# The second layer's sorted feed-forward with its first product turned round, a third turn of store slack, and the loops written out

## The chip, the cores and the metric

The kernel runs on one core of one Trainium2 chip. The metric is the device time of one launch in microseconds (us). The kernel before takes 1609.66 us in the median of three runs (1603.33, 1609.66 and 1609.8).

## The reference

Four layers on 4096 tokens of width 128, each an attention against a context followed by a feed-forward. The change concerns the feed-forward of the second layer (`_L1_ffn_ref`), applied to the normalized x and added to it:

```python
router_probs = softmax(x_flat @ gate_w)                  # 8 experts
expert_idx = argmax(router_probs); expert_w = its probability
for e in range(8):
    h = gelu(x_flat @ w1[e] + b1[e], approximate=False)  # 128 -> 512
    y = h @ w2[e] + b2[e]                                # 512 -> 128
    out = out + where(expert_idx == e, expert_w, 0)[:, None] * y
```

All is float32. Each token needs one expert alone.

## The kernel before, in words

Every engine works through its own list of instructions in order; a `wait_ge` on a semaphore holds back all that stands behind it on that engine. The layer's feed-forward is built by `ffn1` (L1377) in three steps.

`route` computes the gates; its SyncE list loads w1, w2, b1 and b2 (b1 and b2 broadcast to all partitions, L747). `places` (L1087) sorts the tokens by expert on VectorE: each half of the tokens (16 tiles of 128) gets 24 blocks of 128 rows, and every block holds tokens of one expert only, so there are 48 blocks. `c.block_expert` has the expert of each block. `c.expert_pair` (L1184 to L1186) holds two experts in one number, that of a block and that of the block three earlier, for TensorE, which wants both in one turn.

`routed_gelu` (L1189) then runs:

- GpSimd scatters the token rows by indirect DMAs into `slots_x` (L1223, 32 of them). Once a half's results have all been stored it gathers them back from `slots_y` into `c.v` (L1231, 16 a half).
- SyncE loads one block a turn into one of four `xb` buffers (L1245) and stores the result of six blocks earlier (L1248).
- TensorE, in turn i: reads the expert pair from memory into a register (L1272), transposes block i (L1278), multiplies block i-1 with its expert's w1 (L1282: the block is the stationary operand, 512 columns of w1 move, the tokens come out on the partitions), turns the four 128-column parts of the Gelu's result of block i-3 (L1289), and multiplies block i-4 with w2 in four accumulating parts (L1295). Float32 products show as two matmul records each; transposes as one.
- ScalarE copies the transposed block (L1312), copies the turned hidden block (L1316), and takes the Gelu of 128x512 (L1321).
- VectorE adds the broadcast b1 to the 128x512 product (L1337), and b2 to the 128x128 result (L1345). Before each it reads the block's expert into a register (L1334, L1341).
- After its last block VectorE adds the gathered rows to x, times the gate (L1354), takes their statistics (L1358), and aggregates them with one instruction a tile (L1363, 32 of them).

`step` is written out by `run_steps` for the first and last turns and is otherwise a hardware loop of four turns. The lags are in one line:

```python
LAG = dict(X=0, UP=1, HT=3, Y=1 + PAIR_LAG, STORE=6)
```

`moments` (L96) makes mean and variance of all 32 tiles from the statistics with six instructions on all tiles at once (L101 to L109); the other layers use it.

Of the kernel before, what the change touches and what calls it, by code (L numbers as in the profile page):

```python
# [21 lines left out]
P = 128  # L22
# [12 lines left out]
PAIR_LAG = 3  # L35
# [1051 lines left out]
def places(nc, c, d):  # L1087
# [7 lines left out]
    with ExitStack() as own, nc.Block() as block:  # L1095
        numbers, ones, sel, ping, pong, share, over, blocks, ends, ends_b, start, slot, late, ids, pair = scratch(
# [5 lines left out]
                late=([1, HALVES, BLOCKS, EX], F32), ids=([1, HALVES, BLOCKS], F32),  # L1102
                pair=([1, HALVES * BLOCKS + PAIR_LAG], F32)))
# [17 lines left out]
        def _(dve):  # L1121
# [19 lines left out]
            nc.vector.memset(pair[:], 0.0)  # L1141
# [41 lines left out]
            NB = HALVES * BLOCKS  # L1183
            link(nc.vector.tensor_scalar(pair[:, PAIR_LAG:PAIR_LAG + NB], flat_ids, 8.0, None, ALU.mult))  # L1184
            link(nc.vector.tensor_tensor(pair[:, 0:NB], pair[:, 0:NB], flat_ids, ALU.add))
            nc.vector.tensor_copy(c.expert_pair[:], pair[:])  # L1186


def routed_gelu(nc, c, w):  # L1189
# [3 lines left out]
    CH, XB = 4, 4  # L1193
    HT, NB, FF = NT // HALVES, HALVES * BLOCKS, 512
    (xt_psum, xt_ready, h_psum, hb_ready, gelu_ready, ht_psum, ht_ready, y_psum, y_ready, added, stats_ready) = semaphores(
        nc, c, "e1", "xtp xt h hb gelu htp ht yp y add bn")
# [3 lines left out]
    y_out = semaphores(nc, c, "e1", "out0 out1")  # L1200
    xt_bank, h_bank, ht_bank, y_bank = ([c.bank[n], c.bank[n + 1]] for n in (0, 2, 4, 6))
    FIRST, U, LOOPS, LAST = 4, 4, NB // 4 - 1, NB + 6
    LAG = dict(X=0, UP=1, HT=3, Y=1 + PAIR_LAG, STORE=6)
    TB = HT // 4

    def Block(i, r, lag=0):
        return Item(i - lag, r, U, NB)

    with ExitStack() as own, nc.Block() as block:
        xb, xT, hb, h, hT, y, stats = scratch(nc, own, "e1", dict(  # L1210
            xb=([P, XB, P], F32), xT=([P, 2, P], F32), hb=([P, 2, FF], F32), h=([P, 2, FF], F32),
            hT=([P, 2, CH, P], F32), y=([P, 2, P], F32), stats=([P, NT, 6], F32)))

        def rows(halves, a):

            half = a.n // BLOCKS
            return halves[half][bass.ds(a.items(P, -half * BLOCKS * P), P), :]

        @block.gpsimd
        def _(pool):  # L1220
# [4 lines left out]
            for half in range(HALVES):  # L1225
                pool.wait_ge(placed[half], 16 * HT)
                for k in range(2):

                    pool.wait_ge(y_out[k], 16 * (half + 1) * BLOCKS // 2 + 16)
                for j in range(half * HT, (half + 1) * HT):  # L1230
                    nc.gpsimd.indirect_dma_start(c.v[:, j, :], None, c.slots_y[half][:, :],  # L1231
                                                 bass.IndirectOffsetOnAxis(ap=c.slot[:, j:j + 1], axis=0)
                                                 ).then_inc(back[j // TB], 16)

        @block.sync
        def _(sp):
            for s in y_out:
                sp.sem_inc(s, 16)

            def step(i, r):  # L1240
                x, yy = Block(i, r), Block(i, r, LAG["STORE"])
                if x.live:
                    if x.n >= XB:
                        sp.wait_ge(xt_psum, x.items(1, -1))
                    sp.dma_start(xb[:, x.n % XB, :], rows(c.slots_x, x)).then_inc(block_in[x.n % XB], 16)  # L1245
                if yy.live:
                    sp.wait_ge(y_ready, done(yy.t))
                    sp.dma_start(rows(c.slots_y, yy), y[:, yy.b, :]).then_inc(y_out[yy.b], 16)  # L1248

            sp.wait_ge(placed[0], 16 * HT)  # L1250
            run_steps(sp, step, 2 * U, U, BLOCKS // U - 2, BLOCKS)
            sp.wait_ge(placed[1], 16 * HT)
            for i in range(BLOCKS, BLOCKS + 2 * U):
                step(i, 0)
            with sp.Fori(0, BLOCKS // U - 2) as r:
                for n in range(U):
                    step(BLOCKS + 2 * U + n, r)
            for i in range(NB, LAST):
                step(i, 0)
            for s in y_out:  # L1260
                sp.wait_ge(s, 16 * NB // 2 + 16)

        @block.tensor
        def _(pe):
            for s in (xt_psum, h_psum, ht_psum, y_psum):
                pe.sem_inc(s, 2)

            def step(i, r):
                x, up, ht, yy = (Block(i, r, LAG[k]) for k in ("X", "UP", "HT", "Y"))

                if up.live or yy.live:
                    both = pe.value_load(c.expert_pair[0:1, bass.ds(up.t, 1)], min_val=0, max_val=63)  # L1272
                    y_expert = (both >> 3) & 7
                    up_expert = both & 7
                if x.live:
                    pe.wait_ge(block_in[x.n % XB], r * 16 + (16 * (x.n // XB) + 16))
                    pe.wait_ge(xt_ready, free(x.t))
                    nc.tensor.transpose(xt_bank[x.b][:, 0:P], xb[:, x.n % XB, :], c.ident[:]).then_inc(xt_psum, 1)  # L1278
                if up.live:
                    pe.wait_ge(xt_ready, done(up.t))  # L1280
                    pe.wait_ge(hb_ready, free(up.t))
                    nc.tensor.matmul(h_bank[up.b], xT[:, up.b, :],  # L1282
                                     w["w1"][:, bass.ds(up_expert, 1), :].rearrange("d a f -> d (a f)"),
                                     start=True, stop=True).then_inc(h_psum, 1)
                if ht.live:
                    pe.wait_ge(gelu_ready, done(ht.t))
                    pe.wait_ge(ht_ready, free(ht.t))
                    for k in range(CH):
                        last = nc.tensor.transpose(ht_bank[ht.b][:, k * P:(k + 1) * P], h[:, ht.b, k * P:(k + 1) * P], c.ident[:])  # L1289
                    last.then_inc(ht_psum, 1)  # L1290
                if yy.live:
                    pe.wait_ge(ht_ready, done(yy.t))
                    pe.wait_ge(y_ready, free(yy.t))
                    for k in range(CH):
                        last = nc.tensor.matmul(y_bank[yy.b][:, 0:P], hT[:, yy.b, k, :],  # L1295
                                                w["w2"][:, bass.ds(y_expert, 1), k * P:(k + 1) * P].rearrange("d a f -> d (a f)"),
                                                start=k == 0, stop=k == CH - 1)
                    last.then_inc(y_psum, 1)

            run_steps(pe, step, FIRST, U, LOOPS, LAST)  # L1300

        @block.scalar
        def _(act):
            for s in (xt_ready, gelu_ready, ht_ready):
                act.sem_inc(s, 2)

            def step(i, r):
                x, up, ht = (Block(i, r, LAG[k]) for k in ("X", "UP", "HT"))
                if x.live:
                    act.wait_ge(xt_psum, done(x.t))  # L1310
                    act.wait_ge(h_psum, free(x.t))
                    nc.scalar.activation(xT[:, x.b, :], xt_bank[x.b][:, 0:P], ACT.Identity).then_inc(xt_ready, 1)  # L1312
                if ht.live:
                    act.wait_ge(ht_psum, done(ht.t))
                    act.wait_ge(y_psum, free(ht.t))
                    nc.scalar.activation(hT[:, ht.b].rearrange("p k t -> p (k t)"), ht_bank[ht.b],  # L1316
                                         ACT.Identity).then_inc(ht_ready, 1)
                if up.live:
                    act.wait_ge(hb_ready, done(up.t))
                    act.wait_ge(ht_psum, free(up.t))  # L1320
                    nc.scalar.activation(h[:, up.b, :], hb[:, up.b, :], ACT.Gelu).then_inc(gelu_ready, 1)  # L1321

            run_steps(act, step, FIRST, U, LOOPS, LAST)
# [3 lines left out]
        def _(dve):  # L1327
            for s in (hb_ready, y_ready):
                dve.sem_inc(s, 2)

            def step(i, r):
                up, yy = (Block(i, r, LAG[k]) for k in ("UP", "Y"))
                if up.live:
                    e = dve.value_load(c.block_expert[0:1, bass.ds(up.t, 1)], min_val=0, max_val=7)  # L1334
                    dve.wait_ge(h_psum, done(up.t))
                    dve.wait_ge(gelu_ready, free(up.t))
                    nc.vector.tensor_tensor(hb[:, up.b, :], h_bank[up.b],  # L1337
                                            w["b1"][:, bass.ds(e, 1), :].rearrange("p a f -> p (a f)"),
                                            ALU.add).then_inc(hb_ready, 1)
# [678 lines left out]
```

## Time and profile before

| | before |
|---|---|
| median of three runs | 1609.66 us |
| the profiled execution itself | 1602.56 us |
| its span (first to last instruction) | 1600.6 us |
| TensorE matmul busy in the span | 1272.1 us (79%) |
| VectorE busy | 924.9 us (58%) |
| ScalarE busy | 639.6 us (40%) |
| mean granted TensorE clock | 0.86 of 2.4 GHz |
| first block load to last result of the changed loop | 652.4 to 773.8 us of the span |

The profile is of one execution. Busy times of engines overlap, so they don't add up to the span. The chain of waits that ended last covers only the last 40 us of the program (the final sums), so the changed stage must be read from its own stretch of the trace: by the busy time of each engine there, and by what each instruction waited for. DVE is VectorE, ACT is ScalarE, PE is TensorE's matmul and PEld its weight load, POOL is GpSimd, SP is SyncE.

### The profile page before, as it was taken

How to read it: one execution, taken by the hardware profiler on the slowest of the kernel's cores; microseconds unless marked ns; L12 is line 12 of the kernel's file. 1: busy time of each engine (PE TensorE's matmuls, PEld its weight loads, DVE VectorE, ACT ScalarE, POOL GpSimd, SP SyncE). 2: the span in 40 equal slices, each digit the busy share in tenths (PEclk: the TensorE clock that was granted, in tenths of full speed). 3: DMA queues.
4: the chain of work that ended last, by engine and by line, in shares of the span. 5: the costliest groups of instructions: out<-in, count | busy, mean ns of one | idle time of the engine just before them, and what ended most of it. 6: DMA issues, size and time to landing. Idle time of an engine off the chain costs nothing. (4 is left out here: it accounts for less than half of the span.)

```text
span 1600.6 us, 38656 instructions
## 1 busy us (share of the span) xinstructions
PE 1272.1 (79%) x13623; PEld 793.1 (50%) x13624; DVE 924.9 (58%) x2265; ACT 639.6 (40%) x1604; POOL 552.9 (35%) x1109
## 2 busy tenths in 40 slices
PE   3999986998999972699379999966699996864640
PEld 2566655665555552477245555534355555433420
DVE  6566655556677754244564555548657766494324
ACT  1266652222366641355123444431046664442210
POOL 2144412001255412503322334201635422646860
PEclk9799995999899985799688999988879996985555
DMA  5000002800000030212100000010000002142329
GB/s 182 1 3 3 3 2 73 250 1 1 1 2 3 2 157 26 76 54 82 41 1 2 2 2 2 3 54 1 0 2 2 2 2 64 40 171 43 53 36 262
DMA packets 84301, 68.46 MB, mean 43 GB/s; under 512 B 10608, under 2 KB 80048, under 8 KB 82992
## 3 DMA queue, kind: packets, MB, share of 16 engines
q1 hardware_dynamic: 75952, 56.88, 11.5%
q0 software_dynamic: 8192, 9.45, 3.1%
q8 instruction: 103, 1.69, 0.4%
q14 instruction: 54, 0.44, 0.1%
HBM read 42.00 MB, written 24.30 MB: 41 GB/s over the span
## 5 line engine op out<-in xcount | busy, mean ns | idle before, releaser
L481 DVE TENSOR_REDUCE a_m<-psum 128x4 f32<-128x512 f32 x512 | 329.7, 686 | 252.4 <-PE psum L386 99.0
L523 ACT ACTIVATE a_pt<-psum 128x512 f32<-128x512 f32 x512 | 307.2, 601 | 243.0 <-PE psum L414 243.0
L370 PE MATMUL psum<-h_kbd,h_qT 32*128 32x512 f32 x1024 | 323.5, 682 | 23.7 <-PEq L184 21.6
L379 PE MATMUL psum<-h_qbd,h_kT 32*128 32x512 f32 x1024 | 309.8, 659 | 0.0
L423 PE MATMUL psum<-a_pt,v_x 128*32 128x128 f32 x4096 | 165.6, 280 | 2.5 <-ACT a_pvs L531 2.1
L571 POOL CAST max_parts<-a_m 128x16 bf16<-128x16 f32 x128 | 25.1, 196 | 397.5 <-DVE a_m L481 397.5
L414 PEld LDWEIGHTS psum<-a_mt,minus_sb 32*128 32x128 bf16 x2048 | 85.4, 94 | 86.9 <-issue 72.1
L370 PEld LDWEIGHTS psum<-h_kbd,h_qT 32*128 32x128 f32 x1024 | 90.4, 194 | 71.1 <-issue 43.8
L423 PEld LDWEIGHTS psum<-a_pt,v_x 128*32 128x32 f32 x4096 | 96.9, 109 | 30.0 <-issue 4.4
L414 PE MATMUL psum<-a_mt,minus_sb 32*128 32x128 bf16 x2048 | 109.5, 217 | 0.0
L379 PEld LDWEIGHTS psum<-h_qbd,h_kT 32*128 32x128 f32 x1024 | 86.6, 188 | 3.9 <-issue 2.4
L386 PE MATMUL psum<-mask_sb,ident_rows 32*128 32x512 bf16 x1024 | 81.6, 384 | 0.0
L312 PE MATMUL psum<-ident_sb,p_xn 128*128 128x128 f32 x128 | 21.6, 295 | 72.6 <-DVE p_xn L201 72.5
L1337 DVE TENSOR_TENSOR e_hb<-psum,w_b 128x512 f32<-128x512 f32 x48 | 33.2, 692 | 66.8 <-PE psum L1282 66.1
L531 ACT ACTIVATE a_pvs<-psum 128x128 f32<-128x128 f32 x256 | 69.7, 272 | 2.2 <-PE psum L423 2.1
L595 POOL TENSOR_SCALAR h_kbd<-h_kT,head_of 128x512 f32<-128x512 f32 x96 | 65.2, 692 | 0.0
L595 POOL TENSOR_SCALAR h_qbd<-h_qT,head_of 128x512 f32<-128x512 f32 x96 | 65.2, 692 | 0.0
L1231 POOL DMA_INDIRECT v_sb<-slots_y,w_slot x32 | 30.5, 953 | 94.1 <-DMA slots_y<-e_y 84.9
L541 ACT ACTIVATE a_mt<-psum 128x128 bf16<-128x128 bf16 x128 | 35.4, 277 | 68.1 <-PE psum L444 67.0
L312 PEld LDWEIGHTS psum<-ident_sb,p_xn 128*128 128x128 f32 x128 | 16.4, 150 | 89.5 <-DVE p_xn L201 52.9
L386 PEld LDWEIGHTS psum<-mask_sb,ident_rows 32*128 32x128 bf16 x1024 | 34.2, 94 | 52.0 <-issue 38.0
L584 POOL COPY v_x<-v_sb 128x64 f32<-128x64 f32 x256 | 52.0, 236 | 15.2 <-PE psum L423 15.2
(262 smaller groups left out, 2597.2 us busy)
## 6 DMA issues: line engine op xcount, KB each, us to landing
sum_rows<-zero_row SPq DMA_DIRECT2D x1, 8320.0 KB, 37.1
end_sums<-sum_rows SPq DMA_DIRECT2D x16, 512.0 KB, 7.3
w_w<-in_f_w SPq DMA_DIRECT2D x2, 2048.0 KB, 9.9
w_up<-in_f_up SPq DMA_DIRECT2D x1, 4096.0 KB
slots_x<-zero_row SPq DMA_DIRECT2D x2, 1536.0 KB, 9.9
e_xb<-slots_x SPq DMA_DIRECT2D x48, 64.0 KB, 1.8
slots_y<-e_y SPq DMA_DIRECT2D x48, 64.0 KB
x_sb<-in_x SPq DMA_DIRECT2D x4, 512.0 KB, 6.0
```

What stands on the lines that cost most here:

```text
L312: last = nc.tensor.transpose(xt_bank[g % 2][:, j * P:(j + 1) * P], xn[:, g % 2, j, :], c.ident[:])
L370: return nc.tensor.matmul(score_bank[job % 3], c.qT[r, tokens(t)], c.kbd[r, t // GT % 2, :, within(t)], start=True, stop=not masked)
L379: nc.tensor.matmul(turned_bank[job % 3], c.kT[r, tokens(t)], c.qbd[r, t // GT % 2, :, within(t)], start=True, stop=False)
L386: return nc.tensor.matmul(bank, c.ident_rows[r, s, :], c.mask[r, side, s].rearrange("p h k -> p (h k)"), start=False, stop=stop)
L414: last = nc.tensor.matmul(turned_bank[(4 * st + n) % 3][:, j * P:(j + 1) * P], c.minus[r, j, :], mt[r, st % 2, :], start=False, stop=j == 3)
L423: last = nc.tensor.matmul(pv[32 * g:32 * g + 32, f, :], c.vx[:, t % 2, h, :], pt[:, t % 2, h, :], start=odd == 0, stop=odd == 1)
L481: nc.vector.reduce_max(m[:, t % 2, 4 * r:4 * r + 4], score_bank[job % 3].rearrange("p (h k) -> p h k", h=4), AX).then_inc(maxed, 1)
L523: nc.scalar.activation(pt[:, t % 2, 4 * r:4 * r + 4, :].rearrange("p h q -> p (h q)"), turned_bank[job % 3], ACT.Exp, scale=scale).then_in ...
L531: nc.scalar.activation(pvs[:, t % 2, f, :], pv[:, f, :], ACT.Identity).then_inc(pv_ready, 1)
L541: nc.scalar.activation(mt[:, t % 2, :], mt_turned, ACT.Identity).then_inc(mt_ready, 1)
L584: last = nc.gpsimd.tensor_copy(dst[:, :, odd, 16 * odd:16 * odd + HD], src[:, :, odd, :])
L595: last = nc.gpsimd.tensor_scalar(wide[:, g % 2, j, :], of[:, g * GN:(g + 1) * GN], c.head_of[:, j:j + 1], 1.0, ALU.mult, ALU.mult)
```

## The change

The first product is turned round: w1's four 128x128 parts are the stationary operands and the transposed block moves, so the hidden block comes out with its 512 features on the partitions, as the second product needs it. The four transposes of the hidden block and their ScalarE copy go. b1 then lies along the partitions and goes into the Gelu as its bias, four columns behind each expert's w1; the Gelu is four 128x128 instructions that read PSUM. Since the parts of w1 are now stationary operands with fixed addresses, VectorE copies the block's expert (128x516) into one of three `w1` buffers first. The result has three buffers (before two), the hidden block three. TensorE reads one expert a turn (the one for w2); the pairs go. All engines' turns are written out, without a hardware loop. At the end `moments` takes the place of the 32 aggregations.

```diff
 def places(nc, c, d):
...
-            nc.vector.memset(pair[:], 0.0)
...
             nc.vector.tensor_copy(c.block_expert[:], flat_ids)
-            link(nc.vector.tensor_scalar(pair[:, PAIR_LAG:PAIR_LAG + NB], flat_ids, 8.0, None, ALU.mult))
-            link(nc.vector.tensor_tensor(pair[:, 0:NB], pair[:, 0:NB], flat_ids, ALU.add))
-            nc.vector.tensor_copy(c.expert_pair[:], pair[:])
 def routed_gelu(nc, c, w):
-    CH, XB = 4, 4
+    CH, XB, YB, WB, HB = 4, 4, 3, 3, 3
...
+    UP_LAG, Y_LAG = 1, 3
...
+        def stored(b):
+            return 16 * ((b - b % YB) // YB + 1)
...
         def _(sp):
...
+            for b in range(NB + Y_LAG + 2):
+                if b < NB:
+                    if b % BLOCKS == 0:
+                        sp.wait_ge(placed[b // BLOCKS], 16 * HT)
+                    if b >= XB:
+                        sp.wait_ge(xt_psum, b - XB + 1)
+                    sp.dma_start(xb[:, b % XB, :], rows(c.slots_x, b)).then_inc(block_in[b % XB], 16)
+                k = b - Y_LAG - 2
+                if k >= 0:
+                    sp.wait_ge(y_ready, k + 1)
+                    sp.dma_start(rows(c.slots_y, k), y[:, k % YB, :]).then_inc(y_out[k % YB], 16)
...
         def _(pe):
...
+            for i in range(NB + Y_LAG):
+                if i < NB:
+                    pe.wait_ge(block_in[i % XB], 16 * (i // XB + 1))
+                    if i >= 2:
+                        pe.wait_ge(xt_ready, i - 1)
+                    nc.tensor.transpose(xt_bank[i % 2][:, 0:P], xb[:, i % XB, :], c.ident[:]).then_inc(xt_psum, 1)
+                b = i - UP_LAG
+                if 0 <= b < NB:
+                    pe.wait_ge(xt_ready, b + 1)
+                    pe.wait_ge(wide_ready, b + 1)
+                    if b >= 2:
+                        pe.wait_ge(gelu_ready, b - 1)
                     for k in range(CH):
+                        last = nc.tensor.matmul(h_bank[b % 2][:, k * P:(k + 1) * P], w1[:, b % WB, k * P:(k + 1) * P],
+                                                xT[:, b % 2, :], start=True, stop=True)
+                    last.then_inc(h_psum, 1)
+                b = i - Y_LAG
+                if b >= 0:
+                    e = pe.value_load(c.block_expert[0:1, b:b + 1], min_val=0, max_val=7)
+                    pe.wait_ge(gelu_ready, b + 1)
+                    if b >= 2:
+                        pe.wait_ge(y_ready, b - 1)
                     for k in range(CH):
+                        last = nc.tensor.matmul(y_bank[b % 2][:, 0:P], h[:, b % HB, k * P:(k + 1) * P],
+                                                w["w2"][:, bass.ds(e, 1), k * P:(k + 1) * P].rearrange("d a f -> d (a f)"),
                                                 start=k == 0, stop=k == CH - 1)
                     last.then_inc(y_psum, 1)
...
         def _(act):
...
+            for i in range(NB + UP_LAG):
+                if i < NB:
+                    act.wait_ge(xt_psum, i + 1)
+                    if i >= 2:
+                        act.wait_ge(h_psum, i - 1)
+                    nc.scalar.activation(xT[:, i % 2, :], xt_bank[i % 2][:, 0:P], ACT.Identity).then_inc(xt_ready, 1)
+                b = i - UP_LAG
+                if b >= 0:
+                    act.wait_ge(h_psum, b + 1)
+                    if b >= HB:
+                        act.wait_ge(y_psum, b - HB + 1)
+                    for k in range(CH):
+                        last = nc.scalar.activation(h[:, b % HB, k * P:(k + 1) * P], h_bank[b % 2][:, k * P:(k + 1) * P],
+                                                    ACT.Gelu, bias=w1[:, b % WB, FF + k:FF + k + 1])
+                    last.then_inc(gelu_ready, 1)
...
         def _(dve):
...
+            AHEAD = 2
+
+            def take_weights(b):
+                if b >= NB:
+                    return
+                if b >= WB:
+                    dve.wait_ge(gelu_ready, b - WB + 1)
+                e = dve.value_load(c.block_expert[0:1, b:b + 1], min_val=0, max_val=7)
+                nc.vector.tensor_copy(w1[:, b % WB, :], w["w1"][:, bass.ds(e, 1), :].rearrange("p a f -> p (a f)")
+                                      ).then_inc(wide_ready, 1)
+
+            for b in range(AHEAD):
+                take_weights(b)
+            for b in range(NB):
+                take_weights(b + AHEAD)
+                e = dve.value_load(c.block_expert[0:1, b:b + 1], min_val=0, max_val=7)
+                dve.wait_ge(y_psum, b + 1)
+                if b >= YB:
+                    dve.wait_ge(y_out[b % YB], stored(b - YB))
+                nc.vector.tensor_tensor(y[:, b % YB, :], y_bank[b % 2][:, 0:P],
+                                        w["b2"][:, bass.ds(e, 1), :].rearrange("p a f -> p (a f)"),
+                                        ALU.add).then_inc(y_ready, 1)
...
-            for j in range(NT):
-                nc.vector.bn_aggr(c.mv[:, j, :], stats[:, j, :])
+            moments(nc, c, dve, half_mean, links)
 def ffn1(nc, c, d):
...
-                               (b1[:], d["f1_b1"].partition_broadcast(P)), (b2[:], d["f1_b2"].partition_broadcast(P))])
+                               (b2[:], d["f1_b2"].partition_broadcast(P))])
```

The removed engine bodies are those of L1240 to L1349. GpSimd's gathers wait for the last three stores of a half (before: for both result buffers' counts). On the host `f1_w1` gets the four columns of b1 behind each expert's 512.

## Rows read from the trace of the kernel before

**Rows 1.** Two windows of the loop: us, each engine busy (x count), PEclk, DMA

```profile
667.00:720.00 53.00, 52.60 (x331) 39.35 (x330) 21.63 (x44) 28.72 (x66) 3.59 (x4) 1.00 0.21 61
720.00:772.00 52.00, 51.63 (x336) 39.58 (x334) 20.95 (x43) 28.66 (x64) 15.15 (x16) 1.00 0.26 72
```

**Rows 2.** Groups by line in the stretch 655 to 775 us, shapes apart

```profile
L1282 PE MATMUL psum<-w_w,e_xT 128*128 x96 | 52.6, 631 | 1.1 <-DVE e_hb L1337 0.4
L1295 PE MATMUL psum<-w_w,e_hT 128*128 x384 | 50.9, 276 | 0.3 <-issue 0.3
...
L1337 DVE TENSOR_TENSOR e_hb<-psum,w_b 128x512 f32<-128x512 f32 x48 | 33.2, 692 | 66.8 <-PE psum L1282 66.1 <-issue 0.7
...
L1289 PE MATMUL psum<-ident_sb,e_h 128*128 128x128 f32 x192 | 28.8, 273 | 0.0
...
L1312 ACT ACTIVATE e_xT<-psum 128x128 f32<-128x128 f32 x48 | 12.9, 270 | 43.8 <-PE psum L1278 43.8
```

**Rows 3.** Timeline of one turn: start us, us, engine, line, operation

```profile
703.28 0.60 PE L1289 MATMUL psum<-ident_sb,e_h 128*128 128x128 f32 x4
...
703.72 1.06 PE L1295 MATMUL psum<-w_w,e_hT 128*128 x8
...
704.62 0.27 PE L1278 MATMUL psum<-ident_sb,e_xb 128*128 128x128 f32 x1
...
704.72 1.02 PE L1282 MATMUL psum<-w_w,e_xT 128*128 x2
704.92 0.29 DVE L1345 TENSOR_TENSOR e_y<-psum,w_b 128x128 f32<-128x128 f32 x1 [0.51 <-PE psum L1295]
...
705.92 0.69 DVE L1337 TENSOR_TENSOR e_hb<-psum,w_b 128x512 f32<-128x512 f32 x1 [0.71 <-PE psum L1282]
```

**Rows 4.** Timeline where TensorE waited for VectorE, at the loop's start

```profile
660.90 0.69 DVE L1337 TENSOR_TENSOR e_hb<-psum,w_b 128x512 f32<-128x512 f32 x1 [0.46 <-PE psum L1282]
...
661.71 1.12 PE L1282 MATMUL psum<-w_w,e_xT 128*128 x2 [0.41 <-DVE e_hb L1337]
```

**Rows 5.** VectorE's queue at the value load, duration in ns min/median/max

```profile
L1334 DVEq FUSED_REGOPS  x81: 46/190/206, 630.8 to 767.5; - x81
L1334 DVEq TENSOR_LOAD <-w_blockexpert x48: 299/306/552, 630.3 to 767.1; - x48
```

**Rows 6.** VectorE copies and a cast between SBUF tiles, mean ns behind the comma

```profile
L1835 DVE CAST ident_rows<-su_ident_rows 128x512 bf16<-128x512 f32 x1 | 0.4, 421 | 0.0
...
L1134 DVE COPY l_ping<-l_pong 128x128 f32<-128x128 f32 x1 | 0.2, 227 | 0.0
...
L1134 DVE COPY l_pong<-l_ping 128x16 f32<-128x16 f32 x1 | 0.2, 174 | 0.0
```

**Rows 7.** Timeline of the loop's first and last results, and one early product

```profile
655.66 2.07 PE L1282 MATMUL psum<-w_w,e_xT 128*128 x2
...
664.41 0.29 DVE L1345 TENSOR_TENSOR e_y<-psum,w_b 128x128 f32<-128x128 f32 x1 [0.65 <-PE psum L1295]
...
772.04 0.29 DVE L1345 TENSOR_TENSOR e_y<-psum,w_b 128x128 f32<-128x128 f32 x1 [1.27 <-PE psum L1295]
...
773.52 0.29 DVE L1345 TENSOR_TENSOR e_y<-psum,w_b 128x128 f32<-128x128 f32 x1 [1.19 <-PE psum L1295]
```

**Rows 8.** Two other stages, windows with the granted clock

```profile
1076.00:1093.00 17.00, 9.52 (x50) 6.67 (x48) 16.58 (x51) 3.98 (x8) 0.00 (x0) 1.00 0.00 1
1465.00:1543.00 78.00, 51.15 (x146) 35.51 (x146) 28.14 (x100) 18.60 (x73) 62.42 (x48) 0.50 0.35 51
```

**Rows 9.** Block loads of SyncE, issue to landing

```profile
DMA to landing us min/median/max: 1.7/1.8/3.0
```

**Rows 10.** Windows of the pair's, moments' and aggregation's instructions

```profile
629.17:629.80 0.63, 0.00 (x0) 0.00 (x0) 0.55 (x4) 0.00 (x0) 0.00 (x0) 0.50 0.00 0
384.65:385.65 1.00, 0.00 (x0) 0.00 (x0) 0.86 (x7) 0.00 (x0) 0.00 (x0) 1.00 0.00 0
799.70:801.96 2.26, 0.00 (x0) 0.00 (x0) 2.22 (x32) 0.00 (x0) 0.00 (x0) 0.50 0.01 4
```

More of the change, by code:

```diff
@@ L1095, in places @@
     with ExitStack() as own, nc.Block() as block:
-        numbers, ones, sel, ping, pong, share, over, blocks, ends, ends_b, start, slot, late, ids, pair = scratch(
+        numbers, ones, sel, ping, pong, share, over, blocks, ends, ends_b, start, slot, late, ids = scratch(
             nc, own, "l1", dict(
@@ L1101, in places @@
                 endsb=([P, HALVES, EX], F32), start=([P, HALVES, EX], F32), slot=([P, NT], F32),
-                late=([1, HALVES, BLOCKS, EX], F32), ids=([1, HALVES, BLOCKS], F32),
-                pair=([1, HALVES * BLOCKS + PAIR_LAG], F32)))
+                late=([1, HALVES, BLOCKS, EX], F32), ids=([1, HALVES, BLOCKS], F32)))
         @block.sync
@@ L1181, in _ @@
             nc.vector.tensor_copy(c.block_expert[:], flat_ids)
-            NB = HALVES * BLOCKS
-            link(nc.vector.tensor_scalar(pair[:, PAIR_LAG:PAIR_LAG + NB], flat_ids, 8.0, None, ALU.mult))
-            link(nc.vector.tensor_tensor(pair[:, 0:NB], pair[:, 0:NB], flat_ids, ALU.add))
-            nc.vector.tensor_copy(c.expert_pair[:], pair[:])
 def routed_gelu(nc, c, w):
-    CH, XB = 4, 4
+    CH, XB, YB, WB, HB = 4, 4, 3, 3, 3
     HT, NB, FF = NT // HALVES, HALVES * BLOCKS, 512
-    (xt_psum, xt_ready, h_psum, hb_ready, gelu_ready, ht_psum, ht_ready, y_psum, y_ready, added, stats_ready) = semaphores(
-        nc, c, "e1", "xtp xt h hb gelu htp ht yp y add bn")
+    (xt_psum, xt_ready, wide_ready, h_psum, gelu_ready, y_psum, y_ready, added, stats_ready, links) = semaphores(
+        nc, c, "e1", "xtp xt w hp gelu yp y add bn link")
     placed = gpsimd_dma_semaphores(nc, c, "e1", "place0 place1")
@@ L1199, in routed_gelu, with rows @@
     block_in = semaphores(nc, c, "e1", "in0 in1 in2 in3")
[L1200 to L1203, printed above, removed]
+    y_out = semaphores(nc, c, "e1", "out0 out1 out2")
+    xt_bank, h_bank, y_bank = ([c.bank[n], c.bank[n + 1]] for n in (0, 2, 4))
+    UP_LAG, Y_LAG = 1, 3
     TB = HT // 4
-    def Block(i, r, lag=0):
-        return Item(i - lag, r, U, NB)
     with ExitStack() as own, nc.Block() as block:
[L1210 to L1217, printed above, removed]
+        xb, xT, w1, h, y, half_mean = scratch(nc, own, "e1", dict(
+            xb=([P, XB, P], F32), xT=([P, 2, P], F32), w1=([P, WB, FF + CH], F32), h=([P, HB, FF], F32),
+            y=([P, YB, P], F32), hm=([P, 2, NT], F32)))
+        def rows(halves, b):
+            return halves[b // BLOCKS][b % BLOCKS * P:b % BLOCKS * P + P, :]
+        def stored(b):
+            return 16 * ((b - b % YB) // YB + 1)
         @block.gpsimd
@@ L1226, in _ @@
                 pool.wait_ge(placed[half], 16 * HT)
-                for k in range(2):
-                    pool.wait_ge(y_out[k], 16 * (half + 1) * BLOCKS // 2 + 16)
+                for b in range((half + 1) * BLOCKS - YB, (half + 1) * BLOCKS):
+                    pool.wait_ge(y_out[b % YB], stored(b))
                 for j in range(half * HT, (half + 1) * HT):
@@ L1236, in _ @@
         def _(sp):
[L1237 to L1261, printed above, removed]
+            for b in range(NB + Y_LAG + 2):
[9 more added lines that the diff above has]
+                    sp.dma_start(rows(c.slots_y, k), y[:, k % YB, :]).then_inc(y_out[k % YB], 16)
@@ L1263, in _ @@
+            for b in range(NB - YB, NB):
+                sp.wait_ge(y_out[b % YB], stored(b))
         @block.tensor
         def _(pe):
[L1265 to L1287, printed above, removed]
-                    for k in range(CH):
[L1289 to L1293, printed above, removed]
@@ L1298, in step @@
                     last.then_inc(y_psum, 1)
-            run_steps(pe, step, FIRST, U, LOOPS, LAST)
         @block.scalar
         def _(act):
[L1304 to L1321, printed above, removed]
@@ L1327, in _ @@
         def _(dve):
[L1328 to L1339, printed above, removed]
-                if yy.live:
-                    e = dve.value_load(c.block_expert[0:1, bass.ds(yy.t, 1)], min_val=0, max_val=7)
-                    dve.wait_ge(y_psum, done(yy.t))
-                    dve.wait_ge(y_out[yy.b], r * 32 + (yy.n // 2) * 16 + 16)
-                    nc.vector.tensor_tensor(y[:, yy.b, :], y_bank[yy.b][:, 0:P],
-                                            w["b2"][:, bass.ds(e, 1), :].rearrange("p a f -> p (a f)"),
-                                            ALU.add).then_inc(y_ready, 1)
-            run_steps(dve, step, FIRST, U, LOOPS, LAST)
+            AHEAD = 2
[18 more added lines that the diff above has]
+                                        ALU.add).then_inc(y_ready, 1)
             for j in range(NT):
@@ L1956, in host_arrays @@
     f["f1_gate"] = up["gate_w"]
-    f["f1_w1"] = np.ascontiguousarray(up["w1"].transpose(1, 0, 2))
-    f["f1_b1"] = up["b1"]
+    f["f1_w1"] = np.ascontiguousarray(np.concatenate([up["w1"].transpose(1, 0, 2),
+                                                      up["b1"].reshape(8, 4, P).transpose(2, 0, 1)], 2))
     f["f1_w2"] = np.ascontiguousarray(up["w2"].reshape(8, 4, P, P).transpose(2, 0, 1, 3).reshape(P, 8, 512))
```

17 lines of the change are left out of this document (6 added, 11 removed).

## The prediction

> **What bounds the kernel now.** I read first the windows over the changed loop, for the engine that has no idle time there; then the groups by line, for what each instruction costs and what ended the idle time before it; then the timeline of one turn, for the order in which the engines hand a block on. The first view decides: in the two windows TensorE's matmuls are busy 52.6 of 53.0 us and 51.6 of 52.0 us, while VectorE has 21.6 and 21.0 and ScalarE 28.7 in each [rows 1]. So the loop is bound by TensorE, at full granted clock. The groups agree: VectorE's bias add waited 66.1 us for TensorE's first product, and TensorE almost never for anybody [rows 2]. From the first result at 664.41 to the last at 773.52 are 47 turns, 2.32 us each [rows 7].
>
> **One turn of TensorE.** The timeline gives the steps as distances between starts: four transposes of the hidden block 0.44 us (703.28 to 703.72), the second product 0.90 (to 704.62), the transpose of a block 0.10 (to 704.72), and the first product the rest, about 0.86 [rows 3].
>
> **What is removed.** The four transposes, 0.44 us a turn of TensorE; VectorE's add of b1, 692 ns a block [rows 2]; ScalarE's copy of the turned block; the loads of b1. If TensorE stayed the bound, the turn would be 2.32 - 0.44 = 1.88 us. The first product keeps its price: it becomes eight matmul records of 128 columns like the second product's, which take 0.90 [rows 3].
>
> **What is added, and where it lies.** VectorE now copies each block's w1 before TensorE may start the first product (the wait on `wide_ready`). The order on VectorE decides what that costs. It takes two blocks' weights ahead, then alternates: weights of block b+2, result of block b. So the weights of block b+3 are copied right behind the add of b2 for block b. That add needs the second product of block b, which TensorE does last in its turn b+3. And turn b+4 of TensorE needs the weights of block b+3 for its first product. Between the two lies on TensorE only the transpose of a block. So each turn runs through a ring: first product, second product (same turn, TensorE in order), add of b2, copy of weights, next turn's first product. Nothing can run ahead: behind TensorE's wait stand its own second product, and behind that VectorE's add and the next copy; ScalarE, SyncE and GpSimd wait further down.
>
> The ring's terms:
>
> 1. First product's start to second product's start: 0.90 us [rows 3]. TensorE's register load (now between the two) is covered by these 0.90 us of queued matmuls. If nothing covered it, the price is bounded by the last turns of before, where the second product is alone and a turn takes 773.52 - 772.04 = 1.48 us, 0.58 more than its 0.90 [rows 7]. I take 0, since TensorE's queue goes on to the load while the first product still runs; end 0.58.
> 2. Second product's start to the start of VectorE's add: 704.92 - 703.72 = 1.20 [rows 3].
> 3. Start of the add to the start of the copy. In between VectorE's queue loads the expert into a register. Start of an add of b2 to the next VectorE instruction, with the same load between, is 705.92 - 704.92 = 1.00 us, which is the upper end, as it also holds computed addresses and a wait for TensorE [rows 3]. Lower end: the load itself, 0.31, the register operation behind it, 0.19, and one short one of 0.06: 0.56 [rows 5]. I take 0.80, nearer to the row that has the same neighbours.
> 4. The copy, 128x516 float32 within SBUF. Copies of 16 and 128 columns take 174 and 227 ns, 0.47 ns a column, so 0.41 us for 516; a cast of 512 takes 421 ns [rows 6]. Upper end is an add of 512 elements, 0.69 [rows 2]. I take 0.42.
> 5. End of the copy to the next first product: 661.71 - (660.90 + 0.69) = 0.12 us where TensorE waited for VectorE [rows 4]. Ends 0 and 0.20.
>
> Sum: 0.90 + 1.20 + 0.80 + 0.42 + 0.12 = 3.44 us a turn, against 2.32. With all lower ends 3.07, with all upper ones 4.57.
>
> The Trainium skill speaks of term 3 (DMA: Bandwidth & Descriptors, the section on latency and other measured facts): a tensor_load has a floor of about 600 ns. The trace disagrees with 306 ns in the median [rows 5]. By that rule the turn would be 0.3 us longer and the kernel 13 us slower than I forecast.
>
> **The sum.** The first result: first product of block 0 starts at 655.66 as now and takes 2.07 us at the low clock [rows 7], block 1 likewise (less their overlap, 3.7 for both), then at full clock block 2's first product and block 0's second, 1.8, and 0.3 to the add: 661.5. The next 45 results wait for the ring: 45 x 3.44 = 154.8, so 816.3. The last two need no weights: at most 1.48 each [rows 7], 819.3. Against 773.52 that is **+45.8 us**. Behind it stand the stores, the gather of the second half and the adds, all of which start from the last result and are unchanged, so they shift with it.
>
> Small terms: the aggregations take 2.22 us, `moments` with its statistics 0.86 [rows 10], -1.3. The pair's instructions stand on VectorE ahead of the scatter, 0.6 us of window [rows 10], -0.6. The rest I cost at nothing. ScalarE's turn is a copy of 270 ns and four Gelus of the same shape from PSUM, at that price 1.35 us [rows 2], and it has two turns between the first product and its use; if it were slower by half it would still be hidden. Block loads land in 1.8 us, 3.0 at most [rows 9]; SyncE issues them behind a store that waits for a result, which leaves three turns of 3.4 us; stores have three turns to land too. The loads of b1 ran beside routing, which waits for none of them; the written-out code is fetched in turns of 3.4 us with few instructions in each. Bounds for all of these together: 0 to 3 us.
>
> Total +44 us on the profiled execution's own 1602.56 us: 1647. The median of the runs shown is 7 us above that execution and their lowest 1 us, so I put the forecast 3 above: **1650 us**. Its own range by the turn's ends, -0.37 x 45 = -17 and +1.13 x 45 = +51, is 1633 to 1700.
>
> **Rivals.**
>
> - *TensorE's clock falls* (chance 0.16). Now it is never idle in the loop and holds 1.00 [rows 1]. In the ring it works some 1.9 us of 3.44, 55%. For holding: a stage with 9.5 of 17 us busy, 56%, was granted 1.00 throughout. Against: another stage, busy 51 of 78 us, stayed at 0.50 (1.2 GHz) from end to end [rows 8], so once it falls it may not come back. At the low clock a first product takes 2.07 instead of about 1.0 [rows 3, 7], so a turn grows by about 1.9 us: 45 x 1.9 = 86, 1736 us if it holds for the whole loop, 1693 for half of it. The Trainium skill (TensorE: Matmul & The Clock Gate, the part on HAM oscillation) describes such a state: short bursts of matmuls with waits between fall back to the half rate again and again. By that rule the time would be this rival's.
> - *The ring doesn't close, TensorE stays the bound* (0.04). This would need the weights of block b+3 in SBUF before the second product of block b ends, so VectorE's list would have to run ahead of the add, which its order in the diff excludes. Place: TensorE's first product; it decides if the copy ends within the 0.10 us of the transpose. Then a turn is 1.88: 47 x 0.44 = 20.7 less, and 1.9 and some 2.9 of fill less: 1577 + 3 = 1580 us, **faster**.
> - *The register load hides* (0.06). If VectorE's queue loaded the expert while its add still waits for TensorE, term 3 falls to the add's own 0.29 and the turn to 2.93; if the copy also came at the lower end and TensorE's signal sooner, 2.6: 45 x 0.84 = 38 less than forecast, 1612 us, about no change. Against it: the add stands ahead of the load in the queue, and the load's time shows behind it [rows 3, 5].
>
> **Chances.** Forecast 0.74, clock 0.16, hidden load 0.06, TensorE bound 0.04. Differences under 0.5% (8 us) can't be told from none. Slower by more: forecast, clock and half of the hidden load, 0.93; same 0.03; faster 0.04. The range reaches from 1632, leaving the last two cases out below (0.10), to 1697, which leaves out the clock's fall over more than half of the loop (about 0.08).
>
> **What would show it.** In the profile after: results (adds of b2) 3.4 us apart; TensorE's first product idle before it for some 1.5 us a turn, released by VectorE's copy; the copy at about 0.42 us, starting about 0.8 us behind the add; the stage some 46 us longer, all others equal; granted clock 1.00 in the loop. I am wrong if TensorE is busy over 90% of the loop, if the copies run a block ahead of TensorE, or if the clock shows 0.50 for long stretches.

## The result and the profile after

The changed kernel takes 1651.70 us in the median of four runs (1648.91 to 1653.26), the kernel before 1609.73 in the same comparison; the ratio is 1.026, with a 95% interval of 1.0218 to 1.0302. It is slower. The profiled execution of after took 1648.91 us (the fastest of its four runs) with a span of 1646.9, against 1602.56 and 1600.6: the span grew by 46.3 us.

The same view as [rows 1], busy time in a window over the loop of after (us, then PE, PEld, DVE, ACT, POOL busy with their counts, granted clock, DMA share, GB/s):

```profile
662.00:820.00 158.00, 97.42 (x771) 88.13 (x771) 32.84 (x90) 59.90 (x224) 22.06 (x23) 1.00 0.17 47
```

TensorE is busy 97 of 158 us (62%), where it was busy 104 of 105. The granted clock is still 1.00. No other engine is near its limit. So no engine is saturated, and what bounds the loop must be a path through several engines. The groups by line after, as [rows 2]:

```profile
L1257 PE MATMUL psum<-e_xT,e_w 128*128 128x128 f32 x384 | 56.2, 291 | 61.3 <-ACT e_xT L1279 41.3 <-issue 20.0
L1286 ACT ACTIVATE e_h<-psum,e_w 128x128 f32<-128x128 f32 x192 | 54.9, 368 | 101.2 <-PE psum L1257 98.9 <-issue 2.3
L1267 PE MATMUL psum<-w_w,e_h 128*128 x384 | 51.7, 278 | 0.4 <-issue 0.4
...
L1301 DVE COPY e_w<-w_w 128x516 f32 x45 | 19.8, 440 | 21.7 <-issue 21.7
...
L1312 DVE TENSOR_TENSOR e_y<-psum,w_b 128x128 f32<-128x128 f32 x48 | 14.0, 291 | 134.1 <-PE psum L1267 134.1
```

TensorE's first product (L1257) now has 61 us of idle time before it, VectorE's add of b2 (L1312) waits 134 us for the second product (L1267; 28.6 us of it before the very first), and the copy of weights (L1301) 22 us for its own queue. The timeline of one turn, as [rows 3]:

```profile
738.36 0.28 ACT L1279 ACTIVATE e_xT<-psum 128x128 f32<-128x128 f32 x1
738.36 0.29 DVE L1312 TENSOR_TENSOR e_y<-psum,w_b 128x128 f32<-128x128 f32 x1 [2.35 <-PE psum L1267]
...
739.11 0.43 DVE L1301 COPY e_w<-w_w 128x516 f32 x1 [0.47 <-issue]
...
739.64 1.13 PE L1257 MATMUL psum<-e_xT,e_w 128*128 128x128 f32 x8 [1.32 <-issue]
...
740.61 1.06 PE L1267 MATMUL psum<-w_w,e_h 128*128 x8
740.81 1.14 ACT L1286 ACTIVATE e_h<-psum,e_w 128x128 f32<-128x128 f32 x4 [2.18 <-PE psum L1257]
...
741.51 0.27 PE L1249 MATMUL psum<-ident_sb,e_xb 128*128 128x128 f32 x1
741.82 0.29 DVE L1312 TENSOR_TENSOR e_y<-psum,w_b 128x128 f32<-128x128 f32 x1 [2.27 <-PE psum L1267]
```

Follow it as a ring: add (738.36), copy (739.11 to 739.54), first product (739.64), second product (740.61), next add (741.82). The four Gelus beside it (1.14 us) release nothing in this turn, and ScalarE's copy of the transposed block ends at 738.64, 1.00 us before the first product starts. One turn is 3.46 us. The first and last of the 48 results:

```profile
L1312 DVE TENSOR_TENSOR e_y<-psum,w_b x48: 290/292/292, 661.0 to 821.7; 128x128 f32<-128x128 f32 x48
```

From 661.0 to 821.7 are 160.7 us or 3.42 a turn, where [rows 7] had 109.1 and 2.32. These means include the last turns, which are short: without the last two, a turn of after takes 3.51 us.

**Where the 46.3 us come from**, by marks that both traces have: from the first scatter to the first product 24.4 us after, 24.8 before; first product to first result 6.4, before 8.75; first to last result +51.6; last result to the next stage's first VectorE instruction 28.8, before 29.45. With the earlier scatter (-0.7) this gives +47.5 at the start of the next stage; the later stages differ by -1.2.

### The profile page after: what moved, and what is told of

It reads as the page before. It is cut to its first block and busy times, and to the rows that moved or that the text cites. A ratio compares the mean times of both kernels' runs of the same rounds, so it can differ in the third digit from the quotient of the medians.

```text
span 1646.9 us, 37986 instructions
## 1 busy us (share of the span) xinstructions
PE 1262.1 (77%) x13711; PEld 803.1 (49%) x13719; DVE 911.1 (55%) x2234; ACT 640.9 (39%) x1700; POOL 553.8 (34%) x1109
## 5 line engine op out<-in xcount | busy, mean ns | idle before, releaser
L1257 PE MATMUL psum<-e_xT,e_w 128*128 128x128 f32 x384 | 56.2, 291 | 61.3 <-ACT e_xT L1279 41.3
L1286 ACT ACTIVATE e_h<-psum,e_w 128x128 f32<-128x128 f32 x192 | 54.9, 368 | 101.2 <-PE psum L1257 98.9
L1312 DVE TENSOR_TENSOR e_y<-psum,w_b 128x128 f32<-128x128 f32 x48 | 14.0, 291 | 134.1 <-PE psum L1267 134.1
L1257 PEld LDWEIGHTS psum<-e_xT,e_w 128*128 128x128 f32 x384 | 48.6, 198 | 70.9 <-ACT e_xT L1279 58.8
L540 ACT ACTIVATE a_mt<-psum 128x128 bf16<-128x128 bf16 x128 | 35.5, 277 | 68.1 <-PE psum L443 67.5
```

The costliest lines, as they stand in the source:

```text
L540: nc.scalar.activation(mt[:, t % 2, :], mt_turned, ACT.Identity).then_inc(mt_ready, 1)
L1257: last = nc.tensor.matmul(h_bank[b % 2][:, k * P:(k + 1) * P], w1[:, b % WB, k * P:(k + 1) * P], xT[:, b % 2, :], start=True, stop=True)
L1286: last = nc.scalar.activation(h[:, b % HB, k * P:(k + 1) * P], h_bank[b % 2][:, k * P:(k + 1) * P], ACT.Gelu, bias=w1[:, b % WB, FF + k:FF ...
```

## The experiments

Each kernel is compared with the kernel before on the same chip. Since the stage's start alone lies 9 us apart between profiled executions (first scatter at 630.2 after, at 639.3 in the first experiment, in code that both share), I compare the loop from first to last result, one profiled execution of each kernel, and take the totals as the second witness. Two theories: **A**, the ring of the prediction; **B**, that ScalarE's copy of the transposed block, which stands behind four Gelus, holds the first product. B is what the profile's list of waits names (us in total, times, longest), though the timeline above has that copy done early:

```profile
PEld psum L1257 <- ACT e_xT L1279: 58.5, 38, 1.6
PE psum L1257 <- ACT e_xT L1279: 41.3, 31, 1.4
DVE e_w L1301 <- issue: 21.7, 45, 0.8
PE psum L1257 <- issue: 20.0, 14, 1.7
```

**1. Weights three blocks ahead (e1).**

```diff
-            AHEAD = 2
+            AHEAD = 3
```

> One number of the changed kernel differs: VectorE takes the weights three blocks ahead instead of two (AHEAD = 3), still with three buffers. The copy for block b+3 then stands ahead of the add of block b in VectorE's order, so the ring over the add, the register load and the copy is open. Theory A (the ring sets the turn): turns of 1.9 to 2.1 us instead of 3.45, TensorE busy over 90% of the loop, 45 x 1.4 = 63 to 70 us less than the changed kernel's 1652: 1580 to 1590 us. Rival B (what the waits of the profile name: TensorE's first product is released by ScalarE's copy of the transposed block, which stands behind four Gelus): the order on VectorE does not matter, the turn stays at 3.3 to 3.5 us, 1645 to 1655 us.

Measured: 1588.09 us median, ratio to before 0.9848 (0.9812 to 0.9885). Its results and one turn:

```profile
L1312 DVE TENSOR_TENSOR e_y<-psum,w_b x48: 290/292/293, 669.6 to 760.9; 128x128 f32<-128x128 f32 x48
```

```profile
699.81 1.06 PE L1267 MATMUL psum<-w_w,e_h 128*128 x8
699.88 0.43 DVE L1301 COPY e_w<-w_w 128x516 f32 x1 [0.47 <-issue]
...
700.71 0.27 PE L1249 MATMUL psum<-ident_sb,e_xb 128*128 128x128 f32 x1
...
700.81 1.06 PE L1257 MATMUL psum<-e_xT,e_w 128*128 128x128 f32 x8
701.01 0.29 DVE L1312 TENSOR_TENSOR e_y<-psum,w_b 128x128 f32<-128x128 f32 x1 [0.71 <-PE psum L1267]
```

The loop takes 91.3 us. The copy (699.88) runs before the add that it used to follow (701.01), and TensorE goes from the second product to the transpose to the first product without a gap. B falls: ScalarE's order is the same in both kernels. Six of the 47 turns are longer than the usual 1.90 us (2.26 to 2.58); experiment 6 goes into them.

**2. Second product two blocks behind (e2).**

```diff
-    UP_LAG, Y_LAG = 1, 3
+    UP_LAG, Y_LAG = 1, 2
```

> One number differs: the second product runs two blocks behind instead of three (Y_LAG = 2), VectorE's order as in the changed kernel. The copy for block b+3 still stands behind the add of block b, but that add can now start a whole turn of TensorE earlier, so the ring has one turn of slack. Theory A: turns of 1.9 to 2.2 us, 1580 to 1600 us; the Gelus of a block (1.3 us with the signal) have one turn less to finish, but a second product, a transpose and a first product of 1.9 us still lie between. Rival B (ScalarE's copy of the transposed block releases the first product): a shorter lag helps nothing and brings the Gelus nearer, 1650 us or more.

Measured: 1586.40 us, ratio 0.9843 (0.9802 to 0.9883), loop 93.0 us:

```profile
L1312 DVE TENSOR_TENSOR e_y<-psum,w_b x48: 290/292/293, 663.2 to 756.2; 128x128 f32<-128x128 f32 x48
```

VectorE's order is untouched here, so it is the distance between the two stages of the pipeline that counts: "three behind" and "two ahead" are each fine and don't go together.

**3. The register is loaded before the wait (e3).** Each term of the ring can be tried alone. Here the load of the next expert leaves the gap between add and copy; `expert_of` is that load alone.

```diff
+            def expert_of(b):
+                return dve.value_load(c.block_expert[0:1, b:b + 1], min_val=0, max_val=7) if b < NB else None
...
             for b in range(NB):
-                take_weights(b + AHEAD)
+                take_weights(b + AHEAD, ahead)
                 e = dve.value_load(c.block_expert[0:1, b:b + 1], min_val=0, max_val=7)
+                ahead = expert_of(b + 1 + AHEAD)
                 dve.wait_ge(y_psum, b + 1)
```

> The changed kernel, but VectorE reads the expert for the next copy into a register before it waits for TensorE, and not between the add and the copy. Theory A: the distance from the start of the add to the start of the copy falls from 0.76 us to 0.30 to 0.40, the turn from 3.49 to about 3.1, 45 x 0.4 = 18 us less: 1630 to 1638 us. Rival B (ScalarE's copy releases the first product): no change, 1650 us.

Measured: 1634.06 us, ratio 1.0137 (1.0097 to 1.0177), loop 138.2 us.

```profile
700.20 0.29 DVE L1316 TENSOR_TENSOR e_y<-psum,w_b 128x128 f32<-128x128 f32 x1 [2.37 <-PE psum L1267]
700.40 0.42 DVE L1303 COPY e_w<-w_w 128x516 f32 x1
...
700.92 1.13 PE L1257 MATMUL psum<-e_xT,e_w 128*128 128x128 f32 x8 [0.77 <-ACT e_xT L1279]
...
703.14 0.29 DVE L1316 TENSOR_TENSOR e_y<-psum,w_b 128x128 f32<-128x128 f32 x1 [2.31 <-PE psum L1267]
```

Add to copy falls from 0.75 to 0.20 us and the turn from 3.46 to 2.94. The gain in a turn is larger than I expected (0.52 against 0.4), since the copy starts even before the add's record ends. The profile still names ScalarE as the releaser of the first product in this very row (0.77 us), in a kernel where only VectorE's list changed.

**4. Weights copied twice (e4).**

```diff
+                nc.vector.tensor_copy(twice[:, b % WB, :], w["w1"][:, bass.ds(e, 1), :].rearrange("p a f -> p (a f)"))
                 nc.vector.tensor_copy(w1[:, b % WB, :], w["w1"][:, bass.ds(e, 1), :].rearrange("p a f -> p (a f)")
```

> The changed kernel, but VectorE copies each block's weights twice, first into a tile that nobody reads. Theory A: the second copy (0.43 us) lies in the ring, so the turn grows by 0.37 to 0.45 us and the kernel by 45 times that: 1668 to 1673 us. Rival B (ScalarE's copy releases the first product): VectorE has over 2 us to spare in each turn and the second copy hides, 1652 us.

Measured: 1677.12 us, ratio 1.0399 (1.0355 to 1.0444), loop 669.8 to 848.0, 178.2 us.

```profile
703.31 0.29 DVE L1313 TENSOR_TENSOR e_y<-psum,w_b 128x128 f32<-128x128 f32 x1 [2.28 <-PE psum L1267]
...
704.07 0.43 DVE L1301 COPY e_twice<-w_w 128x516 f32 x1 [0.47 <-issue]
704.42 0.42 DVE L1302 COPY e_w<-w_w 128x516 f32 x1
...
707.11 0.29 DVE L1313 TENSOR_TENSOR e_y<-psum,w_b 128x128 f32<-128x128 f32 x1 [2.27 <-PE psum L1267]
```

The second copy starts 0.35 us behind the first and the turn is 3.80: +0.34, all of it in the ring. Over the 45 turns of the ring that is 15 us. The loop grew by 17.5. Most of the rest is a stretch of 6.8 us in which the granted clock was half; two turns there took 5.2 us each, 2.7 us more than two turns at full clock. The median lies 4 us above the range that I had expected.

```profile
680.00:692.00 12.00, 6.62 (x55) 5.99 (x54) 3.17 (x9) 3.96 (x15) 0.07 (x1) 1.00 0.14 40
692.10:698.90 6.80, 5.23 (x25) 4.86 (x25) 1.06 (x3) 2.26 (x9) 0.00 (x0) 0.51 0.07 20
700.00:845.00 145.00, 81.20 (x644) 73.51 (x644) 40.34 (x113) 49.16 (x187) 15.90 (x16) 1.00 0.15 41
```

**5 and 6. Both edits together (e5), and looser loads (e6).** e5 has `AHEAD = 3` and `Y_LAG = 2`. e6 has `AHEAD = 3` and

```diff
-    CH, XB, YB, WB, HB = 4, 4, 3, 3, 3
+    CH, XB, YB, WB, HB = 4, 8, 3, 3, 3
...
-            for b in range(NB + Y_LAG + 2):
+            for b in range(NB + Y_LAG + 4):
...
-                k = b - Y_LAG - 2
+                k = b - Y_LAG - 4
```

> Both single-number edits together: weights three blocks ahead and the second product two blocks behind. Theory A (either edit opens the ring, and TensorE's own 1.9 us a turn is then the bound): nothing more is gained, loop of 90 to 93 us, 1580 to 1590 us. Rival (each edit opened the ring only partly and the rest of the distance to 1.88 us a turn is still VectorE's): both together are 3 us or more below the better of the two, under 1583 us.

> Weights three blocks ahead, and SyncE's order loosened: eight block buffers instead of four, and each store two turns later in SyncE's order, so that a block's load is issued two turns earlier. With the ring open, TensorE still waited for block loads eight times (4 us in all beside the first). Theory A: these waits go, the loop falls from 91.3 to 88 to 90 us, the time to 1580 to 1588 us. Rival (the waits come from landing times that grow while GpSimd's gathers run, not from late issue): same loop length as with three ahead alone.

Measured: e5 1587.24 us, ratio 0.9848 (0.9787 to 0.9909), loop 91.8. Together they give no more than each alone, so either edit opens the whole ring. e6 1583.80 us, ratio 0.9826 (0.9766 to 0.9886). TensorE's transposes idle before them for block loads (total, the stage's first wait included, and times), for e1 and for e6:

```profile
  DMA e_xb<-slots_x: 73.1, 14
```

```profile
  DMA e_xb<-slots_x: 67.7, 3
```

```profile
672.00:755.00 83.00, 83.00 (x742) 82.80 (x741) 32.08 (x87) 56.96 (x217) 21.84 (x23) 1.00 0.31 86
```

Both lists count matmuls and weight loads apart, so one wait can stand in them twice; the stage's first wait alone is 67 us of either. Without it, 5.5 us in 12 records become 0.4 us in one. The loop takes 88.3 us, 1.88 a turn, with TensorE busy 83.0 of 83.0 us. So the waits came from late issue; e6 changes buffers and store order together, and which of the two was needed is not shown. The totals of e1 and e6 overlap within their intervals, so the 3 us rest on the loops, with one profiled execution each.

1.88 is also the value that the prediction gave for a loop bound by TensorE alone, and that is partly luck. A usual turn of e6 is 0.10 + 0.90 + 0.90 = 1.90 us; the prediction took the transposes off but not the 0.04 by which the first product grows (0.86 to 0.90), and its 2.32 was a mean over jumps of the hardware loop and short last turns.

**7 and 10. Four copies (e7) and three (e10)**, one execution each. Their edits are e4's with three or two spare copies.

> The changed kernel with each block's weights copied four times, three of them into tiles that nobody reads. It asks what TensorE's clock does when the ring leaves it idle for most of a turn. Ring alone: a turn of 3.47 + 3 x 0.35 = 4.5 us, loop of about 210 us, kernel about 1700 us. If the clock holds as it does in the changed kernel, all of the loop behind its start shows 1.00. If the idle share of a turn decides (the rival of the prediction), the loop shows 0.50 for long stretches, turns there are 6.2 to 6.5 us, and the kernel takes 1740 us or more.

> As the kernel that copies four times, with three copies: where between two and four copies does the clock begin to go? Ring alone: turn of 3.47 + 2 x 0.35 = 4.17 us, loop of 194 to 197 us. If the fall comes gradually with the idle share: parts of the loop at 0.50, loop of 205 to 225 us. If it holds as with two copies: one short stretch at most, under 200 us.

Measured: e7 1748.05 us, loop 253.2; e10 1738.00 us, loop 664.2 to 909.9, 245.7. Both are far above the ring alone (210 and 195), and e10 is above even its pessimistic range. Stretches of e10, then the whole loop of e10 and of e7:

```profile
679.80:693.40 13.60, 9.79 (x45) 9.04 (x44) 2.79 (x8) 3.98 (x14) 0.00 (x0) 0.50 0.08 21
693.40:696.90 3.50, 1.50 (x13) 1.29 (x13) 1.40 (x4) 0.30 (x2) 0.00 (x0) 0.98 0.14 40
696.90:703.70 6.80, 4.89 (x23) 4.52 (x23) 1.40 (x4) 2.32 (x9) 0.00 (x0) 0.51 0.07 19
703.70:707.10 3.40, 1.40 (x12) 1.19 (x11) 1.40 (x4) 0.49 (x2) 0.00 (x0) 0.98 0.14 39
```

```profile
664.20:909.90 245.70, 156.34 (x779) 142.33 (x779) 63.79 (x183) 64.72 (x227) 23.47 (x24) 0.65 0.11 31
```

```profile
663.50:916.70 253.20, 148.93 (x780) 135.10 (x779) 78.90 (x227) 64.48 (x227) 23.64 (x25) 0.69 0.11 30
```

After the first turns, the granted clock goes back and forth between its two levels, and in e10 the longer stretches are the ones at 0.50 (1.2 GHz). A turn at the low level took 5.9 us where one at full clock took 4.2. One more copy of 0.35 us a turn cost 17.5 us of the loop from one copy to two, 67.5 from two to three, and only 7.5 from three to four. This is the prediction's first rival. It didn't come in the changed kernel, but with 0.34 us more a turn the clock fell once (e4), and with 0.71 more it fell again and again.

**8. The aggregations back (e8)**, one execution: `bn_aggr` for 32 tiles in the place of `moments`.

> The changed kernel with the 32 single aggregations back in place of the six instructions of moments. The prediction put 1.3 us on this: the stretch from the last statistics to the next stage's first VectorE instruction is longer by 1.2 to 1.5 us, the loop is the same. The total will not show it, since runs of one kernel spread over several us.

Measured: 1663.43 us, loop 160.9. The end of the stage, first in the changed kernel, then in e8:

```profile
847.87 0.19 DVE L100 TENSOR_SCALAR e_hm<-stats 128x32 f32<-128x32 f32 x1
...
848.56 0.19 DVE L108 SCALAR_TENSOR_TENSOR mean_var<-mean_var,e_hm 128x32 f32<-128x32 f32 x1
850.51 0.18 DVE L81 TENSOR_SCALAR ln_veps<-mean_var 128x32 f32<-128x32 f32 x1 [1.75 <-PEq L61]
```

```profile
855.46 2.22 DVE L1328 BATCH_NORM_AGGREGATE mean_var<-stats 128x2 f32<-128x6 f32 x32
858.70 0.18 DVE L81 TENSOR_SCALAR ln_veps<-mean_var 128x32 f32<-128x32 f32 x1 [1.02 <-PEq L61]
```

From the first of these instructions to the next stage's first (L81) are 2.64 us and 3.24, not 1.3 apart but 0.60. With `moments` VectorE is done 1.3 us sooner, but then it stands idle for longer before L81: 1.75 us against 1.02, both put down to TensorE's sequencer. What it does there I didn't try. The total of this kernel is some 12 us above the changed kernel's, and this stage doesn't hold them: its first result comes 7.4 us later (668.4 against 661.0), and most of the rest lies in later stages, whose code is the same. So the total of one execution says nothing about the aggregations.

**9. The kernel before, written out (e9).** In `routed_gelu` of the kernel before the four loops of turns become, for instance on TensorE:

```diff
-            run_steps(pe, step, FIRST, U, LOOPS, LAST)
+            for i in range(LAST):
+                step(i, 0)
```

> The kernel before with the turns of this stage written out on all four engines, nothing else. It separates two parts of the change. In the kernel before a turn takes 2.32 us, while the matmuls' own distances sum to 2.30; every fourth turn is longer, where the hardware loop jumps. If the written-out form has a part of its own in the gain of the open-ring kernels: loop of 106 to 108 us instead of 109.1, the time lower by 1 to 3 us. If it has none: 109 us. Theory A puts nearly all the gain of the open ring on the four transposes (20.7 us).

Measured: 1605.86 us, ratio 0.9969 (0.9947 to 0.9992), loop 666.9 to 772.4, 105.5 us.

```profile
670.00:765.00 95.00, 95.00 (x622) 73.31 (x621) 40.79 (x83) 53.05 (x124) 18.65 (x20) 1.00 0.26 72
```

TensorE has no idle time left; writing out is worth 3.6 us of the loop by itself, a little more than I expected (1 to 3). From there to e6's 88.3 are 17.2 us. A usual turn falls from 2.30 to 1.90 us: the transposes (0.44), less the 0.04 by which the first product grows. Over the 44 turns ahead of the short last ones that is 17.6 us.

## Why the prediction was right

- **The ring.** Forecast 3.44 us a turn, measured 3.46 in the timeline. Term by term: first product 0.90, measured 0.97 (739.64 to 740.61; it is 0.90 in e1, where TensorE doesn't wait before it, and why is not shown); second product to add 1.20, measured 1.21; add to copy 0.80, measured 0.75; copy 0.42, measured 0.43; copy to first product 0.12, measured 0.10. Terms 1, 2 and 5 came from distances where one engine really followed another, and those carried over to 0.07 us.
- **What was luck in it.** Term 3 was a choice between 0.56 and 1.00; either end would have moved the kernel by 9 to 11 us. The misses of term 1 (+0.07) and of terms 3 and 5 (-0.05 and -0.02) cancel. The 3 us from the profiled execution to the median were a guess, and 2.8 came.
- **The sign that did not show.** The prediction wanted TensorE's first product released by VectorE's copy in the profile. The idle time is there (1.3 us a turn), but the profile put it down to ScalarE or to "issue"; the timeline and e1 to e4 had to decide.
- **The first and last turns.** First result forecast at 661.5, it came at 661.0. Two misses cancel here: the first product started 1.0 us earlier than in the kernel before (654.6 against 655.66), and from there to the first result took 6.4 us instead of 5.8. The last two, which need no weights, came 1.41 and 1.32 us apart (forecast at most 1.48).
- **The sum.** The last result was forecast 45.2 us later (+45.8, and -0.6 for the pair); it came at 821.68 instead of 773.52, +48.2. The 45 turns of the ring took 3.51 us on average, since some are longer (3.53 to 3.84); that is 2.2 us more than at 3.46, inside the 0 to 3 us that the prediction left open. In the longest, the add starts 1.57 us behind the second product (682.70 and 681.13) instead of 1.21; e8 has the same long turns in the same places, and their cause is open. Pair: -0.6 forecast, -0.66 measured. Aggregation: -1.3 forecast, -0.60 measured (e8); this small term failed, because I took the time that VectorE saves for time that the next stage gains. Span forecast +44, measured +46.3, with -1.2 from later stages in it that nobody forecast.
- **ScalarE.** Priced at 270 ns a Gelu, the records show 368, but they overlap: the four take 1.14 us together, the turn's work is 1.43, and it hides, as forecast, also at 1.9 us a turn.
- **The rival "TensorE stays the bound"** is the state that e1, e2, e5 and e6 reach, once the ring is opened: 1.88 to 1.98 us a turn and 1584 to 1588 us, where the prediction worked out 1.88 and 1580. The order on VectorE excluded it in the changed kernel.
- **The rival "register load hides"** is excluded by the 0.75 us between add and copy, and by e3, which takes the load away and gains it.
- **The rival "clock falls"** did not occur in the changed kernel, but e4, e7 and e10 show that its mechanism is real and near. The prediction's rows could not tell how near, so that it stayed away is partly luck. The rival's price was a little high: a turn at the low level is 1.7 us longer in e10, not 1.9.
- **The disputed figure.** By the Trainium skill's 600 ns for a tensor_load (DMA: Bandwidth & Descriptors, Latency and other measured facts) the forecast turn would have been 3.74 us. The turn of 3.46 decides for the trace's 306 ns, and e3 shows the term by itself: with the load gone, add to copy is 0.55 us shorter, which is the load, the register operation and the short one of [rows 5] (0.31 + 0.19 + 0.06).

## What to carry to other kernels

When work is moved to an engine that also finishes the pipeline, write down for one turn which result each wait needs and in which turn that result is made; if the way back to the start arrives in the same turn, the latencies of all engines on it add up, whatever their busy shares are. Here one number in either of two places (how far ahead the weights are taken, how far behind the second product runs) is worth 64 to 65 us. The version with weights three blocks ahead, eight block buffers and later stores (e6) beats both kernels, at 0.983 of the time before (0.977 to 0.989).

## What the runs showed of the hardware that I had not expected

- **The clock does not go down in proportion to the idle time.** With one copy of weights a turn the granted clock held at 1.00 through the loop; with two it fell once for 6.8 us; with three it was 0.65 on average over the loop, and with four, where TensorE waits longer at full clock, 0.69. So 0.35 us of extra VectorE work a turn cost 17.5, 67.5 and 7.5 us in turn. In e10 TensorE was busy 3.73 of 7.8 us before the clock first fell (672.0 to 679.8), and 9.79 of the 13.6 us at the low level before it rose. Three and four copies were executed once each. The Trainium skill (TensorE: Matmul & The Clock Gate, HAM oscillation) describes such back and forth for bursts of matmuls with DMA waits of 3 to 5 us between; the trace of e10 shows it too, with 0.98 and 0.50 in turn, at shorter waits of about 2 us for another engine. The changed kernel's waits are 1.3 us a turn and its loop kept 1.00, so the prediction went too far when it said that by this description the time would be its rival's.
- **A releaser in the profile can be the wrong one.** Where an instruction waits for several semaphores, the waits named ScalarE's copy of the transposed block, 58.5 us in all, though VectorE's copy of weights ended 0.10 us before the product in each turn of the timeline read. ScalarE's copy had been done for 1.00 us by then (738.64 and 739.64). The experiments (e1 to e4) gave the right name.
- **Records of back-to-back VectorE instructions overlap.** A copy of 0.43 us costs 0.35 when another stands ahead of it (704.07 to 704.42), and a copy starts 0.20 us after an add of 0.29 (700.20 to 700.40).
